# Attention: the row maxima are turned by VectorE and four transfers instead of TensorE transposes and a ScalarE copy

## The reference

```python
qk = jnp.einsum('bdm,bdn->bmn', qh, kh) * scale
sm = jax.nn.softmax(qk, axis=-1)
ret = jnp.einsum('bmn,bcn->bcm', sm, vh)
```

## Time and profile before

| | |
|---|---|
| median of 3 runs | 1624.83 us (1622.52 to 1631.5) |
| profiled execution, span (no other time of it is given) | 1622.8 us |
| TensorE busy | 1524.7 us, 94% |
| VectorE / ScalarE / GpSimd busy | 1189.2 / 981.3 / 1031.2 us |
| mean granted TensorE clock | 0.982 |

### The profile page before, as it was taken

The page is one execution under the profiler, slowest core; times in us unless marked ns, Lnnn a source line. Parts: engine busy times, 40 slices in busy tenths (PEclk is TensorE's granted clock), DMA queues, the critical chain, the costliest instruction groups (busy, mean ns, idle before and its releaser), DMA issues.

```text
span 1622.8 us, 28609 instructions
## 1 busy us (share of the span) xinstructions
PE 1524.7 (94%) x8929; PEld 1067.6 (66%) x8929; DVE 1189.2 (73%) x1868; ACT 981.3 (60%) x1529; POOL 1031.2 (64%) x855
## 2 busy tenths in 40 slices
PE   4999999998887999999999999888999999999996
PEld 3677777777554644444444444378999998999985
DVE  7788888888827777777777776275777777777774
ACT  6433333334724478888888877746777766766773
POOL 3788888885307588888888887502555555555553
PEclk8999999999998999999999999999999999999998
DMA  7344444445763967777776872581444444444443
GB/s 256 108 131 134 136 142 142 142 132 131 207 176 110 211 163 188 200 187 187 198 190 185 201 188 68 178 303 29 78 78 78 79 78 79 79 78 73 75 77 52
DMA packets 111131, 224.27 MB, mean 138 GB/s; under 512 B 12992, under 2 KB 12992, under 8 KB 110144
## 3 DMA queue, kind: packets, MB, share of 16 engines
q1 hardware_dynamic: 94560, 185.10, 40.3%
q0 software_dynamic: 15904, 37.23, 13.2%
q10 hardware_dynamic: 576, 0.79, 0.2%
HBM read 146.71 MB, written 75.84 MB: 137 GB/s over the span
## 4 chain that ended last, share of the span: by engine, by line
PE 33%; DMA 24%; issue 4%; DVE 4%; ACT 2%; POOL 1%; SPq 0%; ACTq 0%; POOLq 0%; DVEq 0%
DMA out_rows<-XN,slots 22%; PE pB L1471 10%; PE pO L1481 8%; PE pA L1453 7%; PE pO L1494 4%; PE pO L1645 1%; DMA XN<-normed_rows,slots 1%; PE pA L1633 1%; PE pB L1462 1%; PE pA L1549 1%; POOL out_rows L1435 1%; DVE low L1827 1%; DVE XN L2010 0%; DMA qs<-q_low 0%; DVE XN L1944 0%
## 5 line engine op out<-in xcount | busy, mean ns | idle before, releaser
L1827 DVE TENSOR_REDUCE low<-pA 128x2 f32<-128x1024 f32 x256 | 307.0, 1223 | 109.4 <-PE pA L1453 95.8
L1722 ACT ACTIVATE pt<-pB 128x512 f32<-128x512 f32 x512 | 287.7, 594 | 89.7 <-PE pB L1471 81.1
L1435 POOL DMA_INDIRECT out_rows<-XN,slots x71 | 196.9, 2773 | 217.9 <-DMA out_rows<-XN,slots 170.1
L436 PE MATMUL y<-kv,toep 128*128 128x288 f32 x1280 | 326.0, 411 | 9.0 <-DVEq L63 5.8
L436 PEld LDWEIGHTS y<-kv,toep 128*128 128x128 f32 x1280 | 238.0, 190 | 96.8 <-DVEq L63 34.0
L1633 PEld LDWEIGHTS pA<-XN,fc 128*128 128x128 f32 x2272 | 265.6, 192 | 10.9 <-issue 5.6
L1633 PE MATMUL pA<-XN,fc 128*128 128x128 f32 x2272 | 266.4, 276 | 5.0 <-DVE XN L1990 4.0
L1471 PE MATMUL pB<-qs,ks 98*128 98x512 f32 x512 | 226.9, 446 | 3.3 <-ACT pt L1722 2.4
L1471 PEld LDWEIGHTS pB<-qs,ks 98*128 98x128 f32 x512 | 95.6, 188 | 192.2 <-ACT pt L1722 149.2
L406 ACT ACTIVATE ym<-y 128x384 f32<-128x384 f32 (+1 forms) x128 | 52.6, 411 | 228.9 <-PE y L436 228.9
L1787 ACT ACTIVATE proj_high<-WP 128x2048 fp32r x71 | 135.7, 1912 | 83.6 <-PE pO L1645 83.6
(11 more groups left out here) (294 smaller groups left out, 2448.4 us busy)
## 6 DMA issues: line engine op xcount, KB each, us to landing
ks<-ctx_high SPq DMA_DIRECT2D x62, 256.0 KB, 4.6
qs<-q_high SPq DMA_DIRECT2D x62, 256.0 KB, 6.1
kc<-in_ctx_conv SPq DMA_DIRECT2D x32, 384.0 KB, 5.5
XN<-in_x SPq DMA_DIRECT2D x16, 512.0 KB, 9.8
toep<-kernel_and_skip SPq DMA_DIRECT2D x32, 256.0 KB, 3.5
ct<-in_ctx SPq DMA_DIRECT2D x16, 512.0 KB, 6.6
ctx_high<-kh SPq DMA_DIRECT2D x16, 512.0 KB, 4.5
ctx_low<-kl SPq DMA_DIRECT2D x16, 512.0 KB, 5.2
```

The lines of the kernel that those rows point to most:

```text
L436: m = pe.matmul(y[half].rearrange("p (l n) c -> p l n c", l=CB)[:, l, :, 0:PAIRS], toep[u][:, (l - s) * P:(l - s + 1) * P], kv[u][:, half, ...
L1435: pool.indirect_dma_start(out=out["out"], out_offset=bass.IndirectOffsetOnAxis(ap=slots[:, j:j + 1], axis=0), in_=ys[j % 2], in_offset=Non ...
L1722: act.activation(pt[s][:, h, :], bank(u, n), ACT.Exp, scale=SCALE1).then_inc(s_exp, 1)
L1827: dve.tensor_reduce(ap(low[u % 2], t % CB * NH + t // CB, [[NH, 2], [1, 1]]), pA[n % 2], op=ALU.max, axis=AX.X, negate=True).then_inc(s_re ...
```

## The change

VectorE now does the splitting and the turning. `halves` moves from GpSimd to VectorE, is called behind the last reduction of each unit, and ends with one `transpose` of `split` (128 x 32) into `turned`. This works on blocks of 32 x 32: partition 32n + r of `turned` then holds the 32 queries of group n of tile r (r below 16 the high part, above it the low part). `shift` sends four transfers, one for each group n of 32 partitions, in pieces of 32 numbers, straight to the two spare rows of `qs`. `maxima` and `keep` go, and with them the 17th place in the ring of `pB` banks; `tops` goes; the counts of the semaphores follow. The new `halves` waits for the previous unit's transfers before it writes `turned`. The wait of the first reduction of a unit on `s_sp` goes.

```diff
             def shift(j, u):
-                sp.wait_ge(s_exp, made(j - 1, TURN) if not isinstance(j, int) or j > 0 else 1)
-                for row in range(2):
-                    part = tops[row * NH:(row + 1) * NH]
-                    sp.dma_start(qs[u][NS + row:NS + row + 1], bass.AP(part.tensor, part.offset, [list(part.ap[0]), [C, 1], [1, C]])).then_inc(s_md, 16)
+                sp.wait_ge(s_sp, 3 * j + 3)
+                for n in range(P // HD1):
+                    rows = qs[u][NS:NS + 2].rearrange("r h m -> r (h m)")
+                    sp.dma_start(ap(rows, n * HD1, [[P, NH * CB], [1, HD1]]),
+                                 ap(turned[n * SQUARE:(n + 1) * SQUARE], 0, [[HD1, 1], [1, HD1]])).then_inc(s_md, 16)
...
-            def halves(j, u):
-
-                pool.wait_ge(s_red, DUOS * j + DUOS)
-                wait(pool, s_b, made(j - 2, TURN) if not isinstance(j, int) or j > 1 else j)
-                pool.sem_inc(s_go, 1)
-                pool.tensor_copy(split[:, :, 0:NH].bitcast(F32R), low[u % 2]).then_inc(s_sp, 1)
-                pool.wait_ge(s_sp, 2 * j + 1)
-                pool.tensor_tensor(split[:, :, NH:].bitcast(F32R), low[u % 2], split[:, :, 0:NH], ALU.subtract).then_inc(s_sp, 1)
-                pool.wait_ge(s_sp, 2 * j + 2)
...
-            def maxima(j, to):
-
-                pe.wait_ge(s_sp, 2 * j + 2)
-                for k in range(CB):
-                    t = pe.transpose(to[0:2 * NH, k * P:(k + 1) * P], split[:, k, :], ident)
-                t.then_inc(s_b, 1)
...
-                    if beat in (2, 5, 13):
+                    if beat in (2, 5, FAR, 13):
                         score(*ahead(j, i, u, beat))
-                    if beat == TURN and exists(j + 1):
-                        score(*ahead(j, i, u, beat))
-                        wait(pe, s_exp, made(j, TURN - 2))
-                        maxima(j + 1, bank(u, TURN))
                     second(j, u, beat // NH, beat % NH)
...
-            def keep(j, rows, count):
-
-                act.wait_ge(s_b, count)
-                if not isinstance(j, int) or j > 0:
-                    act.wait_ge(s_md, 32 * j)
-                act.activation(tops.bitcast(F32R), rows[0:2 * NH, :], ACT.Copy).then_inc(s_exp, 1)
...
+            def halves(j, u):
+
+                dve.wait_ge(s_red, DUOS * j + DUOS)
+                dve.tensor_copy(split[:, 0:TILES].bitcast(F32R), low[u % 2]).then_inc(s_sp, 1)
+                dve.wait_ge(s_sp, 3 * j + 1)
+                dve.tensor_tensor(split[:, TILES:].bitcast(F32R), low[u % 2], split[:, 0:TILES], ALU.subtract).then_inc(s_sp, 1)
+                wait(dve, s_md, SHIFTS * j)
+                dve.sem_inc(s_go, 1)
+                dve.wait_ge(s_sp, 3 * j + 2)
+                dve.transpose(turned, split).then_inc(s_sp, 1)
+
             def reduce(j, i, u, n):
                 if not exists(j):
                     return
-                if n == 0:
-                    wait(dve, s_sp, 2 * j - 2)
                 dve.wait_ge(s_a, DUOS * j + n + 1)
-                t = 2 * n
-                dve.tensor_reduce(ap(low[u % 2], t % CB * NH + t // CB, [[NH, 2], [1, 1]]), pA[n % 2], op=ALU.max, axis=AX.X, negate=True).then_inc(s_red, 1)
+                dve.tensor_reduce(low[u % 2][:, 2 * n:2 * n + 2], pA[n % 2], op=ALU.max, axis=AX.X, negate=True).then_inc(s_red, 1)
+                if n == DUOS - 1:
+                    halves(j, u)
```

More of the change, by code:

```diff
@@ L1058, in _build @@
     ROOTED = 7
+    SQUARE = 2 * NH * CB
     CONSTANTS = ROOTED + 9 + E1 + 1
@@ L1066, in _build @@
         lns, inv, att = (sb(under, n, [P, C]) for n in ("lns", "inv", "att"))
-        tops = sb(under, "tops", [2 * NH, C])
         nextq, nexth, nextl = (sb(under, n, [P, C]) for n in ("nextq", "nexth", "nextl"))
@@ L1084, in _build @@
     with ExitStack() as st:
-        low = [sb(st, f"low{i}", [P, CB, NH]) for i in range(2)]
-        split = sb(st, "split", [P, CB, 2 * NH])
+        low = [sb(st, f"low{i}", [P, NH * CB]) for i in range(2)]
+        split = sb(st, "split", [P, 2 * NH * CB])
+        turned = sb(st, "turned6", [P, SQUARE])
         ones = sb(st, "ones6", [P, HD1])
@@ L1164, in _build @@
         TILES = NH * CB
+        SHIFTS = 16 * P // HD1
         DUOS = TILES // 2
-        RING = TILES + 1
-        TURN = 10
+        FAR = 10
         LEAD = 5
@@ L1190, in following, with place @@
             return j + n, i + (u + n) // TRIP, (u + n) % TRIP
[L1192 to L1198, removed]
+        def place(s, h):
+            return NH * s + h
         def made(j, n):
-            return RING * j + n + 2
+            return TILES * j + n + 1
         def wait(eng, signal, count):
@@ L1251, in body @@
                     if before:
-                        sp.wait_ge(s_b, made(j - 1, place(j - 1, CB - 1, NH - 1)))
+                        sp.wait_ge(s_b, made(j - 1, place(CB - 1, NH - 1)))
                         sp.sem_inc(s_go, 1)
@@ L1297, in _ @@
             sp.wait_ge(s_sum, 2 * UNITS)
-            sp.wait_ge(s_md, 32 * UNITS)
+            sp.wait_ge(s_md, SHIFTS * UNITS)
             for e in range(E1 - 1):
@@ L1391, in body @@
                     query_low(j + 4)
-                if exists(j + 1):
-                    halves(j + 1, (u + 1) % TRIP)
-                pool.wait_ge(s_exp, made(j, place(j, 1, NH - 1)))
+                pool.wait_ge(s_exp, made(j, place(1, NH - 1)))
                 wait(pool, s_sum, 2 * j - 1)
@@ L1399, in body @@
                     pool.wait_ge(s_add, 4 * j + n + 1)
-                pool.wait_ge(s_exp, made(j, place(j, 2, NH - 1)))
+                pool.wait_ge(s_exp, made(j, place(2, NH - 1)))
                 for n in range(2):
@@ L1408, in _ @@
             rows_roots()
-            halves(0, 0)
             constants()
@@ L1456, in score @@
                     m.then_inc(s_a, 1)
-            def maxima(j, to):
-                pe.wait_ge(s_sp, 2 * j + 2)
-                for k in range(CB):
-                    t = pe.transpose(to[0:2 * NH, k * P:(k + 1) * P], split[:, k, :], ident)
-                t.then_inc(s_b, 1)
             def second(j, u, s, h):
-                n = place(j, s, h)
+                n = place(s, h)
                 if s == 0 and h == 0:
-                    pe.wait_ge(s_md, 32 * j + 32)
+                    pe.wait_ge(s_md, SHIFTS * j + SHIFTS)
                 wait(pe, s_exp, made(j, n - 2))
-                pe.matmul(bank(u, n), ks[u][0:NS + 2, h, s * P:(s + 1) * P].bitcast(F32R), qs[u][0:NS + 2, h, :].bitcast(F32R),
+                pe.matmul(pB[n % 2], ks[u][0:NS + 2, h, s * P:(s + 1) * P].bitcast(F32R), qs[u][0:NS + 2, h, :].bitcast(F32R),
                           start=True, stop=True).then_inc(s_b, 1)
@@ L1478, in values @@
                     wait(pe, s_ln, j)
-                pe.wait_ge(s_exp, made(j, place(j, s, NH - 1)))
+                pe.wait_ge(s_exp, made(j, place(s, NH - 1)))
                 for h in range(NH):
@@ L1487, in sums @@
                 if last:
-                    pe.wait_ge(s_exp, made(j, place(j, CB - 1, NH - 1)))
+                    pe.wait_ge(s_exp, made(j, place(CB - 1, NH - 1)))
                 else:
@@ L1510, in body @@
                 for beat in range(TILES):
-                    if beat in (2, 5, 13):
+                    if beat in (2, 5, FAR, 13):
                         score(*ahead(j, i, u, beat))
-                    if beat == TURN and exists(j + 1):
-                        score(*ahead(j, i, u, beat))
-                        wait(pe, s_exp, made(j, TURN - 2))
-                        maxima(j + 1, bank(u, TURN))
                     second(j, u, beat // NH, beat % NH)
-                    if beat not in (2, 5, TURN, 13):
+                    if beat not in (2, 5, FAR, 13):
                         score(*ahead(j, i, u, beat))
@@ L1532, in _ @@
                     stir(pe, idle, 3)
-            maxima(0, pB[1])
             pe.wait_ge(s_one, 6)
@@ L1719, in body @@
                     for h in range(NH):
-                        n = place(j, s, h)
+                        n = place(s, h)
                         act.wait_ge(s_b, made(j, n))
-                        act.activation(pt[s][:, h, :], bank(u, n), ACT.Exp, scale=SCALE1).then_inc(s_exp, 1)
+                        act.activation(pt[s][:, h, :], pB[n % 2], ACT.Exp, scale=SCALE1).then_inc(s_exp, 1)
                         if NH * s + h == 2 and exists(j + 4):
@@ L1730, in body @@
                             norm(j - 4, i - 1, u)
-                        if NH * s + h == TURN - 1 and exists(j + 1):
-                            keep(j + 1, bank(u, TURN), made(j, TURN))
-                        if NH * s + h == TURN and exists(j - 1):
+                        if NH * s + h == FAR and exists(j - 1):
                             logarithm(j - 1, u - 1)
-                        if NH * s + h == TURN + 2 and exists(j - 1):
+                        if NH * s + h == FAR + 2 and exists(j - 1):
                             inverse(j - 1)
```

(1 more changed line is left out.)

## The result

| | median | runs |
|---|---|---|
| before | 1626.63 us | 8, 1622.32 to 1631.5 |
| changed | 1630.86 us | 8, 1628.99 to 1635.5 |

The medians differ by 4.2 us. The ratio is 1.0035 with a 95% interval of 1.0019 to 1.0051, so 3 to 8 us more; forecast was no measurable change, at 1625 us. The interval leaves out zero, so the changed kernel is slower, but by less than the 0.5% that the forecast took as the least it could tell. The profiled execution has a span of 1628.9 us against 1622.8.

A forecast was written before the change was run, and what follows sets the result against it. TensorE was taken as full, with VectorE equally long from beat 1 to 10. Steady units +3.1 us, other units and start -4.0, rounded to about 0: profiled span 1622.8, plus 2.0 for the median, 1625 us; range 1612 to 1638.

The forecast's parts named there:

- the likeliest case: Whole kernel: no measurable change, TensorE's gain and VectorE's loss cancel, 1620 to 1631 us; chance 0.60.
- VectorE's stretch: Attention unit, beats 1 to 10: VectorE runs operations without slack up to the reduction that beat 10's score matmul needs.
- the units that were to gain: Units 0 to 3 -1.9, unit 30 -0.5, start of unit 1 -1.7, load of unit 2 +0.1: sum -4.0 us.
- The bound: Steady attention unit: TensorE full for 15.2 us, VectorE as long from beat 1 to 10, so added work there lengthens it.
- The extension of 0.60: VectorE, beats 1 to 10: three operations add 0.70 us, a lost wait gives back 0.10; bounds 0.45 to 1.2.
- The 0.48 of the transposes: TensorE at beat 10: removing four transposes saves 0.48 us a unit, read from beat 10 against beat 13.
- Net per steady unit: Units 4 to 29: 0.60 added less 0.48 saved gives +0.12 us each, 26 units +3.1 us.
- the 1.7 us for unit 1's wait for its transfers: Second matmul of unit 1: waits of 1.3 on the weight load and 0.4 on the matmul go, -1.7 us.
- rival 3: Beat 0 of each unit: transfers come late and it waits 0.9 us, some +25 us, 1650 us; chance 0.08.
- rival 2: VectorE's stretch: transpose of 0.72 makes the extension 1.12, VectorE the clear bound, +12.6 us, 1638 us; chance 0.20.
- (b): VectorE's stretch has slack, its additions are hidden, all 31 units give 0.48: -16.6 us, 1608 us; chance 0.05.
- (a): VectorE's stretch: the three operations overlap as unwaited ones do, extension 0.16, -12 us, 1613 us; chance 0.07.

The follow-up runs named there:

- e3: Changed kernel with copy, subtraction and transpose done a second time into unused tiles, right behind the first: 1654.59 us, ratio 1.0190.
- e5: Changed kernel with `measure` moved from beat 5 to beat 9, splitting and turning left at beat 5: 1612.81 us, ratio 0.9927.
- e9: Kernel before the change, with only `measure` moved from beat 5 to beat 9: 1624.02 us, ratio 1.0005.
- e6: Changed kernel with `measure` at beat 9, plus four transposes with unused results on TensorE at beat 10: 1624.10 us, ratio 0.9996.
- e11: Kernel before the change, run once more unedited for a second profile: 1627.44 us.
- e10: Changed kernel, run once more unedited for a second profile: 1629.57 us.
- e2: Changed kernel with VectorE's splitting and turning moved from beat 5 to beat 9: 1659.13 us, ratio 1.0211.
- e4: Changed kernel with splitting and turning at beat 7, plus four transposes with unused results on TensorE at beat 10: 1626.05 us, ratio 1.0012.
- e1: Changed kernel with VectorE's splitting and turning moved from beat 5 to beat 7: 1625.19 us, ratio 1.0007.
- e7: Changed kernel with splitting and turning at beat 7 and the rounding copy made by a `tensor_reduce`: 1616.0 us, one run.

## Why the prediction held, and where it was off

The time was 1630.86, inside the range and inside the half per cent of the likeliest case, but above its point by 6 us, of which 1.8 are the longer series of runs of before (1626.63 for 1624.83). The mechanism held: TensorE saved what was forecast and VectorE's stretch took more than that back. Gain and loss did not cancel, though, and the 1630.86 stands at the upper edge of the 1620 to 1631 of that case. Its own formula gives, with the extension that was measured, 26 x 0.20 - 4 = +1: the missing part is in the units that were to gain. The steps:

- **The bound.** That VectorE had no slack between beats 1 and 10, so that work put there counts one for one, is shown by e3 (+0.72 for a set counted at 0.65 to 0.75, which in its timeline takes 0.75) and e5 (-0.68 when as much or more is taken out).
- **The extension of 0.60.** From the end of the second reduction to the stats it went from -0.09 to +0.70 (785.60 to 786.30), so 0.79 where 0.70 stood, and the gap in front of the next reduction fell from 0.35 to 0.24, the 0.10 that was allowed. Extension 0.68. The transpose at 0.21 and the copy and subtraction at 0.175 were sized right; the gap in front of the transpose was 0.13 instead of 0.07. The unit of e5, which has no stall, confirms the sum: 15.39 - 14.71 = 0.68.
- **The 0.48 of the transposes.** It was right: 0.47 between e9 and e5. Four transposes put back by themselves cost 0.40 (e6), because the second behind them takes 0.23 and not 0.30; the reading of beat 10 against beat 13 had taken in the whole of it.
- **Net per steady unit.** +0.12 was forecast, +0.21 to +0.23 measured, and 0.68 - 0.47 = 0.21: 24 units gave about +5.3 instead of +2.9. Nearly all of it is the extension, mis-sized by 0.08.
- **The units that were to gain.** This is the part of the prediction that failed. -4.0 us were credited; -0.5 came, at the end, and up to unit 4 the two kernels differ by +0.2, with 1 us of scatter, where -3.5 stood. Two reasons show. First, units 2 and 3 have no `refine`, and I took its 0.98 us as cover. But in them the reduction behind it waits for TensorE anyway (1.00 us in the row below, from unit 3 of the changed kernel; 1.01 in the same place before), so the stretch without slack begins at beat 3 and `refine` had only filled a gap. They still waited for VectorE and took 15.2 and 15.1 us where e5 has 14.9 and 14.8; they gained 0.13 to 0.15 each, not 0.48. Second, the 1.7 us for unit 1's wait for its transfers added one wait twice. The 1.3 on the weight load and the 0.4 on the matmul of the earlier trace rows are the same wait of the same matmul, and TensorE was idle for 0.4 of it; in e11 there was none at all. And it did not go: 0.6 us in the changed kernel, 1.9 in e10. The pieces went out earlier, 23.6 us after the first reduction of the stage instead of 27.5, but close behind the loads of unit 3 on the same queue, the last of which landed at 563.41; in the chain of the changed kernel they land 9.67 us after the start of the last issue, where 4.61 stood in the earlier trace rows.

```profile
598.75 2.35 DVE L1798 TENSOR_REDUCE low<-pA 128x2 f32<-128x1024 f32 x2 [1.00 <-PE pA L1438]
601.14 0.17 DVE L1786 CAST split<-low 128x16 fp32r<-128x16 f32 x1
```

```profile
555.51 9.67 DMA qs<-turned
```

- **The rivals.** Late transfers (rival 3) show once per execution, at unit 1, and not in the steady units, where 1.3 us from the end of the issue are enough (e2). A transpose in four passes (rival 2) is refuted by its row, 0.21. Of the faster cases, (b) falls with e3, and (a), an extension of 0.16, with the 0.68. (a) was what the Trainium skill's rule (VectorE: DVE Perf Modes, The DRAIN you can't avoid) would give. The set of e3 takes 0.75 from the start of its copy to that of the next (813.02 to 813.77), with 0.56 of work in it, so 0.19 pass between operations each of which waits for the one before. No run leaves these waits out, so what they alone cost is not shown.

What the change lost was room on VectorE at one place. With `measure` moved to beat 9 it beats both kernels: 1612.81 us, 0.7% below the one before, and the 0.47 a unit that the prediction had read is then there in full.

## What to carry to other kernels

Busy shares show the fullest engine, but a ring of two banks ties two engines together at every handover: look for a run of operations without an idle entry on the less busy engine, and take from there what need not be there before adding to it. When a block is moved, look at what the neighbour engine does at the new place as well; a copy of 16 elements cost eight times its time beside a GpSimd sum. And when a variant does not move the time, put the removed work back into it: that the transposes were free in e4 said that the bound was elsewhere, not that they are free. A wait that is listed for the weight load and again for its matmul is one wait; only the matmul's idle time is lost.

## What the runs showed that was not expected

- A VectorE copy of 128x16 took 1.37 us at beat 7 and 2.17 at beat 9 instead of 0.175 while GpSimd added tiles in SBUF; a reduction of the same size took 0.16 in the same place (e1, e2, e7).
- TensorE's granted clock fell to 0.50 within unit 0, after the waits for transfers at the start of the stage, in both kernels (e11; the first profile of the changed one). Waits and clock fall now ahead of unit 0, now inside it: it took 12.4 to 18.5 us in the profiles of all variants, while from the first reduction of the stage to unit 4 both kernels stay within 78.7 to 79.8.
- A single unit of e3 took 7 us more than its neighbours: one subtraction held for 2.33 us, a wait of 3.59, and a granted clock of 0.50 for the 8 us behind it.
- Four transfers of 4 KB needed 1.3 us after the end of the last issue in the steady units and 9.1 us at the start (556.1 to 565.2), behind the loads of whole units on the same queue.
